# Attention with routed experts on one core: transposes of rows and logits, the first experts' inputs and a unit's row maxima rearranged

## What is computed

```
x = L0_attn_x
x = _layernorm(x + _L0_attn_ref(x, W_dq, W_uq, W_dkv, W_uk, W_uv, W_o))
x = _layernorm(x + _L0_ffn_ref(x, w_router, wi, wo))
```

## Time and profile before

| what | us |
|---|---|
| runs | 589.47, 589.88, 592.38 |
| profiled execution, device time | 590.35 |
| its span, first to last instruction | 588.5 |
| PE busy | 525.7 |
| DVE busy | 442.9 |
| ACT busy | 354.1 |

### The profile page before, as it was taken

One profiled execution on the slowest core, in us unless ns is written; L12 is line 12 of the kernel. 1 busy time (PEld: TensorE's weight loads), 2 busy tenths in 40 slices (PEclk: granted clock), 3 DMA queues, 4 the chain that ended last, 5 costly groups with the idle time before them and its releaser, 6 DMA issues.

```text
span 588.5 us, 10326 instructions
## 1 busy us (share of the span) xinstructions
PE 525.7 (89%) x3491; PEld 217.9 (37%) x3491; DVE 442.9 (75%) x1300; ACT 354.1 (60%) x719; POOL 63.2 (11%) x64
## 2 busy tenths in 40 slices
PE   4967999899999998989989999989999999955991
PEld 2523333233333333224545333333223222223891
DVE  3687999898888979976757878988888872445616
ACT  0613556656667765664765777667777779934231
POOL 9400000000000000450000460000000000000031
PEclk9966999999999999998999999999999999985996
DMA  3379991300000300010000160000000000000024
GB/s 87 120 225 232 200 279 51 58 2 2 2 1 2 82 1 1 29 64 6 1 13 1 37 48 3 1 3 0 1 2 2 1 2 10 19 9 1 0 41 55
DMA packets 25410, 24.90 MB, mean 42 GB/s; under 512 B 2314, under 2 KB 22668, under 8 KB 25356
## 3 DMA queue, kind: packets, MB, share of 16 engines
q1 hardware_dynamic: 21660, 20.42, 13.7%
q0 software_dynamic: 1280, 2.62, 3.8%
q10 hardware_dynamic: 2416, 1.18, 0.7%
HBM read 16.81 MB, written 7.28 MB: 41 GB/s over the span
## 4 chain that ended last, share of the span: by engine, by line
PE 59%; issue 20%; DVE 11%; DMA 3%; POOL 3%; ACT 2%; SPq 0%; ACTq 0%; DVEq 0%; POOLq 0%
PE acc L1106 16%; PE ring L1067 15%; PE ring L1089 13%; DVE part_max L789 3%; POOL exp_in L579 3%; DVE unused L794 2%; PE ring L1093 2%; PE ms L1170 2%; DMA qT<-maxT 1%; PE ms L1197 1%; PE ms L1191 1%; PE ring L1184 1%; PE ring L1197 1%; PE ring L1191 1%; DVE x L865 1%
## 5 line engine op out<-in xcount | busy, mean ns | idle before, releaser
L662 ACT ACTIVATE probs<-ring 128x512 f32<-128x512 f32 (+3 forms) x560 | 268.5, 536 | 136.4 <-PE ring L1093 74.0
L789 DVE TENSOR_REDUCE part_max<-ring 128x1 f32<-128x512 f32 x384 | 254.4, 686 | 45.1 <-PE ring L1067 42.1
L1067 PE MATMUL ring<-kT,qT 126*128 126x512 bf16 (+3 forms) x640 | 221.6, 360 | 10.0 <-DVE part_max L794 4.5
L1089 PE MATMUL ring<-qT,kT 128*128 128x512 bf16 (+3 forms) x640 | 214.5, 352 | 4.0 <-DMA qT<-maxT 3.2
L1106 PE MATMUL acc<-probs,v 128*9 128x512 f32 (+3 forms) x1280 | 147.6, 533 | 0.9 <-ACT yT L673 0.9
L794 DVE CUSTOM_DVE_ANT_0 unused<-ring,causal 128x128 bf16<-128x128 f32 (+3 forms) x256 | 120.3, 483 | 20.3 <-PE ring L1067 18.0
L1067 PEld LDWEIGHTS ring<-kT,qT 126*128 126x128 bf16 x640 | 61.9, 98 | 178.7 <-DVE part_max L789 102.5
L1089 PEld LDWEIGHTS ring<-qT,kT 128*128 128x128 bf16 x640 | 61.9, 99 | 46.7 <-ACT probs L660 15.7
L1093 PE MATMUL ring<-later,ident 128*128 128x128 bf16 x256 | 55.4, 221 | 0.0
L1106 PEld LDWEIGHTS acc<-probs,v 128*9 128x9 f32 x1280 | 19.0, 88 | 50.6 <-issue 25.7
L660 ACT ACTIVATE probs<-ring 128x1024 f32<-128x1024 f32 (+3 forms) x40 | 33.2, 900 | 2.8 <-issue 1.6
(11 more groups left out here) (179 smaller groups left out, 341.1 us busy)
## 6 DMA issues: line engine op xcount, KB each, us to landing
kT<-parts_k SPq DMA_DIRECT2D x9, 384.0 KB
qT<-parts_q SPq DMA_DIRECT2D x9, 384.0 KB
wi<-in_L_ffn_wi SPq DMA_DIRECT2D x1, 2048.0 KB, 18.5
parts_k<-wi SPq DMA_DIRECT2D x3, 384.0 KB, 3.6
parts_q<-wi SPq DMA_DIRECT2D x3, 384.0 KB, 4.8
kT<-parts_k SPq DMA_DIRECT2D x12, 96.0 KB
qT<-parts_q SPq DMA_DIRECT2D x12, 96.0 KB
x<-in_L_attn_x ACTq DMA_DIRECT2D x4, 256.0 KB, 4.4
```

The lines of the kernel that those rows point to most:

```text
L662: nc.scalar.activation(probs[:, at, 0:width], ring[:, bank, 0:width], ACT.Exp).then_inc(exp_done, 1)
L789: nc.vector.tensor_reduce(dst, sc[i % SRING][:, :], AX.X, ALU.max).then_inc(sc_used, 1)
L1067: nc.tensor.matmul(sc[i % SRING][:, 0:w], qT[s % 2][0:MROW, head, qt * P:(qt + 1) * P], kT[0:MROW, head, c * QUERIES:c * QUERIES + w], sta ...
L1089: ins = nc.tensor.matmul(bank[:, 0:QUERIES - off], kT[:, head, j * P:(j + 1) * P], qT[s % 2][:, head, off:QUERIES], start=True, stop=True, ...
```

## The change

The row transposes and the logits of blocks 0, 1 and 2 come two steps later (x1_turn from steps 25, 57 and 105 to 27, 59 and 107, logits one step behind each). The tasks top2, count and slots of the first group come two steps later (from 59 and 60 to 61 and 62). The first experts' inputs (`in_turn`) come four steps later than that, in all six (from 68 and 69 to 74 and 75), and the first group's experts and `send_back` move with them (experts from 70 to 85 to 76 to 91, `send_back` from 87 to 93). The last block and the second group stay where they are.

A unit's maxima are laid out as value or remainder, head, query tile, so that one transpose turns all 32 columns into 32 partitions of 128. ACT copies 32 x 128 instead of 8 x 512, and the transfer writes the same 8 KB in 32 runs of 128 bf16 values instead of 8 runs of 512.

```diff
         b = FIRST[GROUPS * (s + 1)] + 3
         for q in range(QT):
             out.append((b + q, "y_turn", QT * s + q))
-        out += [(b + 4, "norm_ln", ("attn", s)), (b + 5, "norm_out", ("attn", s)), (b + 6, "x1_turn", s), (b + 7, "logits", s)]
+        out += [(b + 4, "norm_ln", ("attn", s)), (b + 5, "norm_out", ("attn", s))]
+        b += 2 * (s < SUPERS - 1)
+        out += [(b + 6, "x1_turn", s), (b + 7, "logits", s)]
     for g in range(MOE_GROUPS):
-        b = FIRST[2 * GROUPS * (g + 1)] + 3 + 8
+        b = FIRST[2 * GROUPS * (g + 1)] + 3 + 8 + 2 * (g < MOE_GROUPS - 1)
         out += [(b, "top2", g), (b + 1, "count", g), (b + 1, "slots", g)]
-        b += 9 if g < MOE_GROUPS - 1 else 2
+        b += 13 if g < MOE_GROUPS - 1 else 2
...
-        max16 = [sb(f"max16_{i}", [P, QT, 2, HG], BF16) for i in range(2)]
-        maxT = [sb(f"maxT{i}", [2 * HG, QUERIES], BF16) for i in range(2)]
+        max16 = [sb(f"max16_{i}", [P, 2, HG, QT], BF16) for i in range(2)]
+        maxT = [sb(f"maxT{i}", [2 * HG * QT, P], BF16) for i in range(2)]
...
-                nc.scalar.activation(maxT[u % 2][:, :], bank.bitcast(BF16)[0:2 * HG, 0:QUERIES], ACT.Copy).then_inc(maxT_kept, 1)
+                nc.scalar.activation(maxT[u % 2][:, :], bank.bitcast(BF16)[0:2 * HG * QT, 0:P], ACT.Copy).then_inc(maxT_kept, 1)
...
-                act.dma_start(qT[super_of(u) % 2][MROW:MROW + 2, g * HG:(g + 1) * HG, :], maxT[u % 2][:, :]).then_inc(max_in[u % 2], 16)
+                rows = qT[super_of(u) % 2][MROW:MROW + 2, g * HG:(g + 1) * HG, :]
+                act.dma_start(rows.rearrange("a h (q t) -> a h q t", t=P), maxT[u % 2][:, :]).then_inc(max_in[u % 2], 16)
...
-                nm = neg_max[:, :].rearrange("p (q h) -> p q h", q=QT)
-                link(nc.vector.tensor_copy(m[:, :, 0, :], nm))
-                nc.vector.tensor_tensor(m[:, :, 1, :], nm, m[:, :, 0, :], ALU.subtract).then_inc(max_done, 1)
+                nm = neg_max[:, :].rearrange("p (q h) -> p h q", q=QT)
+                link(nc.vector.tensor_copy(m[:, 0, :, :], nm))
+                nc.vector.tensor_tensor(m[:, 1, :, :], nm, m[:, 0, :, :], ALU.subtract).then_inc(max_done, 1)
...
                 pe.wait_ge(max_done, u + 1)
-                for q in range(QT):
-                    ins = nc.tensor.transpose(bank.bitcast(BF16)[0:2 * HG, q * P:(q + 1) * P],
-                                              max16[u % 2][:, q, :, :].rearrange("p a h -> p (a h)"), ident16[:, :])
-                return ins
+                return nc.tensor.transpose(bank.bitcast(BF16)[0:2 * HG * QT, 0:P],
+                                           max16[u % 2][:, :, :, :].rearrange("p a h q -> p (a h q)"), ident16[:, :])
```

## The result

The changed kernel takes 583.86 us in the median of 12 runs (581.17 to 588.29), the kernel before 589.49 in 12 runs beside it (588.43 to 592.38): a ratio of 0.9912, with a 95% interval of 0.9892 to 0.9932. The forecast was 583.8. A second set of runs gave 584.66 (6 runs) against 588.94 (10), a ratio of 0.9927 (0.9904 to 0.9951). The profiled execution took 584.08 us, with a span of 582.3.

A forecast was written before the change was run, and what follows sets the result against it. PE sets the pace in undisturbed attention, DVE some 13 to 17% below. Terms -2.9 - 0.9 - 0.4 - 2.4 + 0.5 = -6.1 us bring the median from 589.88 to 583.8 us, range 580.8 to 589.2.

The forecast's parts named there:

- The experts' inputs: Moved six steps later: steps 68 to 73 -8.1, 86 to 91 +6.3, 74 and 75 about -1.1; sum -2.9 us.
- the 1.7 us of the clock's fall: After in_turn's wait in step 68: 14 us at clock 0.88 instead of 1.00 cost 1.7 us.
- Block 0: x1_turn moved to step 27: 0.4 of a 1.18 us wait and 0.3 gained, 1.3 lost to a meeting; +0.6 us.
- Block 1: PE's 1.13 us wait for normalized rows, gain bounded by 0 and 1.13; -0.7 us taken, no new meeting.
- Block 2: Wait for rows -1.25, max_turn's wait -0.31, new meeting at step 107 +1.3; sum -0.3 us.
- The single transpose: One transpose for four of a unit's maxima: 0.24 us saved in ten of fifteen units, -2.4 us.
- The meetings: Turns behind a max_turn wait for shared PSUM bank: three new at 1.3 us each; steps 19, 79, 91 cheaper, -0.9.
- The start: Unit 0's maxima transfer, in 32 shorter pieces, takes about a microsecond longer but is issued some 0.6 us earlier: +0.5 us.
- The first, waits that only change their name: Rival: freed PE meets DVE's ring, meetings cost 1.6, transposes vanish behind DVE; -0.8, 589.1 us; chance 0.20.
- The second: Rival: unit 0's transfer, issued 0.6 us sooner, precedes the load of queries; the 3.22 us wait goes; 580.1 us; chance 0.08.
- The third, short pieces: Rival: short pieces in the crowded queue stretch unit 0's transfer to 20.9 us, 12.5 more; 595.8 us; chance 0.06.
- The fourth: Rival: each of three new meetings lowers the clock, at 1.7 us each; 588.9 us; chance 0.04.

The follow-up runs named there:

- the runs at steps 72 and 70: Changed kernel with the first in_turn at step 72, or 70, instead of 74; single executions took 584.48 us (72) and 591.12 (70).
- loads_held: Changed kernel with SP holding back block 1's loads until unit 0's maxima have landed; 583.47 us in 4 runs, 0.9901.

## Why the prediction was right in its time, and where its steps failed

**The experts' inputs** are the step that carried the result, and it was right: -8.1 forecast and -8.2 measured in steps 68 to 73 (24.43 to 16.27), +6.0 and +6.31 in 86 to 91 (the 0.3 for the cheaper meeting counted in), -1.1 and -1.2 in 74 and 75. The clock is 1.00 throughout. The load was issued 9.3 us ahead of in_turn (267.03 and 276.29), and the runs at steps 72 and 70 put the end of the cover between them. One piece was counted too certainly: the 1.7 us of the clock's fall. At in_turn a wait of 2.69, 2.74 or 3.70 us was followed by it in three profiles, and a wait of 2.93 was not in one; the wait of 2.00 us in step 4 of loads_held was followed by it too.

**Block 0** is the step that failed: "only part of 1.18 counts; bounds 0 and 1.18, I take 0.4". Nothing of it counted. The mechanism was the one named there, DVE's ring, but the value was the lower bound. The sign to decide by was in the trace of before. PE's wait lies in step 25, and there DVE is busy for 4.95 of 4.98 us; the pause of 1.28 us that ends at 139.22 lies in step 26, where PE is busy throughout, with the logits among its work (windows of before, steps 25 and 26):

```profile
131.99:136.97 4.98, 3.80 (x27) 1.61 (x26) 4.95 (x17) 4.14 (x9) 0.00 (x0) 1.00 0.00 0
136.97:139.77 2.80, 2.80 (x22) 1.33 (x21) 1.52 (x7) 1.35 (x4) 0.00 (x0) 1.00 0.00 0
```

With the meeting the block costs 1.5 us instead of 0.6. **Block 1** has the same fault in small, -0.4 for -0.7. **Block 2** came out right, -0.2 for -0.3 (steps 105 and 106 gave 2.5 us, steps 107 and 108 took 2.3 back), but two of its terms were off and nearly cancelled. The wait of 1.25 us for the rows went. The 0.31 in front of max_turn did not go: it is now a wait for DVE's maxima, in the row of step 107 shown with the result. And the meeting took 1.08 us instead of 1.3.

**The single transpose** was mis-sized twice, -1.0 for -2.4 (-1.3 with what stands in other rows). I divided 0.32 by four. In the trace of before the four stand only 0.056 us apart, and the next matmul follows the last of them by 0.15 us; it follows a single one by 0.17, so a turn saves 0.16. And of the ten turns eight saved it: six by themselves, and those of steps 91 and 107 inside the rows of the experts and of block 2. In the meetings of steps 19, 27 and 79 nothing is saved, because the copy begins when ACT is free, 0.60 to 0.64 us behind the start of the transposes in both kernels.

**The meetings** wait 1.40 to 1.44 us in steps 19, 27 and 79 instead of 1.3, for the same reason: some 0.4 us pass from the end of the transpose to the copy (139.63 - 1.43 = 138.20 to 138.60). In steps 91 and 107 they wait 1.08, so that the five make 6.4 us, nearly 5 x 1.3: right in the sum, by errors both ways. The copy's 0.25 was right, and steps 19 and 79 gained the 0.3 that was forecast.

**The start.** I added 0.5 us for short pieces. From issue to unit 0's first score, the old shape took 8.48, 9.97 and 10.08 us in three profiles (9.5 in the mean); the new one took 8.65 to 11.02 in eight (9.6). No run shows a price for the pieces, and where nothing is in the way there is none: by the semaphores in the traces, the transfers of units 5 to 11 land 1.91 to 2.13 us after their issue in 8 pieces (before) and 1.90 to 2.06 in 32 (changed). The issue comes 0.8 us earlier in the mean (40.96 to 40.12), and the first value matmul 0.7 us earlier (58.5 to 57.8). The 2.0 us between the first two profiles are therefore mostly that pair's own: unit 0's maxima were ready 1.2 us sooner there, ahead of anything the change touches. The tail runs from 67.4 to 73.0 us over all profiles; three of the old kernel's shape are too few to tell an order. So what I would now forecast for the change is -3.6 - 0.7 = -4.3 us, with the 0.7 an estimate from starts that scatter by more than that. The second set of runs moved by 4.3 us (588.94 to 584.66), the first by 5.6; the interval of the first, 0.9892 to 0.9932 of 589.49, spans 4.0 to 6.4 us and holds it. Of the 5.6 us by which the forecast was met, 1.3 are not accounted for by the change.

**The rivals.** The first, waits that only change their name, was true of block 0, of the 0.31 us in block 2 and partly of the transposes, not of the rest. The second failed by its own condition: in the changed kernel the transfer is issued ahead of the load of queries (39.72 and 40.60), and PE still stands 3.07 us for it. Only with the keys held back as well was unit 0 free. The third, short pieces, did not occur. The rule of the Trainium skill ("DMA: Bandwidth & Descriptors", Specifications), at least 512 bytes in a piece for full rate, shows no effect on the time of this transfer of 8 KB inside SBUF, neither among the loads (9.5 and 9.6 us to the first use) nor alone (about 1.95 us in both shapes). The fourth did not occur either: the clock stayed at 1.00 through every meeting of 1.4 us.

**Left open:** why the clock fell after three of the four waits of in_turn and after the shorter one of loads_held, which of block 1's loads holds up unit 0's transfer, what shifts the clock's low stretches in the tail, and whether the meeting in step 79 can be moved as well, which was not tried.

## What to carry to other kernels

A wait that is moved away is only gained where no other engine's limit stands close behind it: look at whether that engine pauses in the very step where the wait lies; a pause one step on is no sign of room. When turns share a bank, price each new pair of neighbours in it from the moment at which the copying engine is free, and let the engine that copies release the bank before it issues a transfer. Where whole runs scatter by more than a term is worth, measure the term between two marks of the program that repeat.

## What the runs showed of the hardware that I had not expected

- A single transpose of 128 x 32 takes 0.17 us until the next matmul starts, four of 128 x 8 take 0.32: one is half of four, not a quarter, since the four follow one another by 0.056 us and the next matmul by 0.15.
- The clock's fall does not follow the length of PE's wait alone: 2.00, 2.69, 2.74 and 3.70 us were followed by it, 2.93 us was not.
- From the issue of unit 0's transfer to its first use 8.5 to 11 us pass, in 32 pieces or in 8. With the loads of block 1 held back it lands within 2.1 us.
